# Epsilon inside the variance sums, scores on four quarters of the array, two columns more in one product, and another order of steps

## What is computed

```python
# layer 0: graph convolution, two dense layers, each with a norm over all 8192 rows
# layer 1: layernorm, attention with 4 heads, layernorm, MLP, layernorm
xp = einsum('mn,bnf->bmf', L_norm, x)
x1 = relu(_layernorm(xp @ Wc + bc, g1, be1)) + x
scores = einsum('bhnd,bhmd->bhnm', q, k) / sqrt(hd)        # hd = 64
attn = softmax(where(adjacency > 0, scores, -1e9))
o = einsum('bhnm,bhmd->bhnd', attn, v)
x2 = _layernorm(x1 + o @ Wo + bo, g2, be2)
y = _layernorm(x2 + gelu(x2 @ W1 + b1) @ W2 + b2, g3, be3)
# layer 2: two graph convolutions, then LSTMs over windows of 1, 2, 3, 4 nodes
# layer 3: graph attention
Wh = einsum('bnf,fo->bno', h, W)
s1, s2 = Wh @ a1, Wh @ a2
e = s1[:, :, None] + s2[:, None, :]        # leaky relu, mask, softmax
h_prime = einsum('bij,bjo->bio', attention, Wh)
# every layernorm: (x - mean) / sqrt(var + eps), here over 256 features
```

## Time and profile before

| | |
|---|---|
| median of three runs | 2094.58 us (2092.04 to 2097.44) |
| the profiled execution | 2096.32 us, of which the profile's span is 2094.5 us |
| PE busy | 1982.5 us, 95% |
| DVE busy | 1774.0 us, 85% |
| ACT busy | 1448.0 us, 69% |
| first and second part | 0 to 243 us |
| opening | 243 to about 373.6 us |
| seven rounds | about 225.5 us each, to 1951.9 us |
| closing | 1951.9 us to 2094.5 us |

### The profile page before, as it was taken

One profiled execution on the slowest core, in us unless ns is written; L12 is line 12 of the kernel. 1 busy time (PEld: TensorE's weight loads), 2 busy tenths in 40 slices (PEclk: granted clock), 3 DMA queues, 4 the chain that ended last, 5 costly groups with the idle time before them and its releaser, 6 DMA issues.

```text
span 2094.5 us, 86503 instructions
## 1 busy us (share of the span) xinstructions
PE 1982.5 (95%) x37415; PEld 1754.9 (84%) x37415; DVE 1774.0 (85%) x5049; ACT 1448.0 (69%) x4411; POOL 189.0 (9%) x252
## 2 busy tenths in 40 slices
PE   6999879999999999999999999999999999999997
PEld 3444469989898989899998989898989999899996
DVE  6769787889888988898888988898889888988866
ACT  5657436767776677767776777677776777677776
POOL 2000010110101000101011110101010101111000
PEclk9999989999999999999999999999999999999999
DMA  7847300000100001000100010000100010000000
GB/s 280 292 166 282 129 9 15 13 12 3 43 3 23 3 3 43 13 13 3 43 13 12 3 43 3 23 3 5 42 13 13 3 43 13 13 4 12 3 3 23
DMA packets 36825, 87.84 MB, mean 42 GB/s; under 512 B 2416, under 2 KB 26992, under 8 KB 32752
## 3 DMA queue, kind: packets, MB, share of 16 engines
q1 hardware_dynamic: 36464, 82.56, 11.4%
HBM read 52.15 MB, written 30.41 MB: 39 GB/s over the span
## 4 chain that ended last, share of the span: by engine, by line
PE 65%; DVE 14%; ACT 8%; issue 2%; POOL 0%; DVEq 0%; ACTq 0%
PE ps L283 19%; PE ps L285 18%; PE ps L284 18%; DVE stats L1610 2%; PE ps L297 2%; ACT pool_mem L1486 2%; PE ps L1226 2%; PE ps L1144 2%; PE ps L1135 1%; DVE pool_mem L1764 1%; ACT hl_a L1502 1%; DVE mv L1614 1%; PE ps L1381 1%; DVE t L1810 1%; PE ps L1251 1%
## 5 line engine op out<-in xcount | busy, mean ns | idle before, releaser
L1486 ACT ACTIVATE pool_mem<-ps,lstm_b 128x64 f32<-128x64 f32 (+2 forms) x2496 | 607.7, 357 | 95.6 <-PE ps L285 94.6
L283 PE MATMUL ps<-hl_a,w_hi 128*128 128x64 f16 (+2 forms) x3776 | 540.2, 214 | 16.9 <-DVE hl_a L654 15.9
L284 PE MATMUL ps<-hl_a,w_hi 128*128 128x64 f16 (+2 forms) x3776 | 539.3, 214 | 0.0
L285 PE MATMUL ps<-hl_a,w_lo 128*128 128x64 f16 (+2 forms) x3776 | 539.0, 214 | 0.0
L283 PEld LDWEIGHTS ps<-hl_a,w_hi 128*128 128x128 f16 x3776 | 349.1, 97 | 44.9 <-DVE hl_a L654 17.1
L285 PEld LDWEIGHTS ps<-hl_a,w_lo 128*128 128x128 f16 x3776 | 348.9, 97 | 23.7 <-issue 1.9
L284 PEld LDWEIGHTS ps<-hl_a,w_hi 128*128 128x128 f16 x3776 | 348.9, 97 | 22.6 <-issue 1.6
L283 PE MATMUL ps<-hl_b,w_hi 128*128 128x84 f16 (+2 forms) x2112 | 366.2, 228 | 1.0 <-DVE hl_b L1662 1.0
L284 PE MATMUL ps<-hl_b,w_hi 128*128 128x84 f16 (+2 forms) x2112 | 366.3, 228 | 0.0
L285 PE MATMUL ps<-hl_b,w_lo 128*128 128x84 f16 (+2 forms) x2112 | 364.4, 228 | 0.0
L284 PE MATMUL ps<-pool_mem,w_hi 128*128 128x64 f16 (+2 forms) x3072 | 351.1, 200 | 0.6 <-issue 0.6
(11 more groups left out here) (234 smaller groups left out, 4339.6 us busy)
## 6 DMA issues: line engine op xcount, KB each, us to landing
xa<-in_x SPq DMA_DIRECT2D x32, 512.0 KB, 5.5
h_scratch<-pool_mem SPq DMA_DIRECT2D x14, 1024.0 KB, 4.3
pool_mem<-h_scratch SPq DMA_DIRECT2D x14, 1024.0 KB, 7.0
...
```

Source lines behind the costliest of these rows:

```text
L283: nc.tensor.matmul(o, l[0], r[0], start=first, stop=False, skip_group_check=True)
L284: nc.tensor.matmul(o, l[0], r[1], start=False, stop=False, skip_group_check=True)
L285: return nc.tensor.matmul(o, l[1], r[0], start=False, stop=last, skip_group_check=True)
L1486: op = nc.scalar.activation(gates[s][h][:, g, m * w:(m + 1) * w], gate_place(s, h, g, m, w), ACT.Tanh, bias=lstm_b[:, bias:bias + 1], scal ...
```

## The change

Four things are changed.

**Epsilon.** The statistics buffer has nine columns a block instead of six. The three new ones hold 0, 0 and 256 x epsilon from the start on, and `bn_aggr` reads all nine, so that its variance comes out with epsilon in it. The addition on DVE is gone, and POOL takes the power of `mv` directly. The waits between `bn_stats`, `bn_aggr`, centring and scaling are now for each block instead of for both.

**Scores.** The second pair of heads writes to the opposite partitions and to the half's other bank, so that the 16 products use the four quarters in turn.

**Attention vectors.** They are stored as columns 256 and 257 behind the matrix W3 (`w3a`), and the 12 matmuls of `gat` have 258 columns. The 12 matmuls of two columns are gone. Block `b` of a half now has a bank to itself. ACT takes the parts out, in a new small instruction ahead of the copy of Wh, and the addition of DVE's L1785 is gone. `gat_keys` waits for the copy of Wh, because it writes into the bank that the copy reads.

**Order.** All three tables are written anew.

The core of the diff:

```diff
-        mask1 = sb("mask1", [P, NODES])
+        mask1 = sb("mask1", [P, P])
-        wa = sb("wa", [P, 2, KT, 2], F16)
+        w3a = sb("w3a", [P, 2, KT, DIM + 2], F16)
-        stats = [sb(f"stats_{s}", [P, BLK, 6]) for s in range(STREAMS)]
+        stats = [sb(f"stats_{s}", [P, BLK, 9]) for s in range(STREAMS)]
...
+                for s in range(STREAMS):
+                    nc.gpsimd.memset(stats[s][:, :, 6:8], 0.0)
+                    nc.gpsimd.memset(stats[s][:, :, 8:9], DIM * EPS)
...
+                for half, of in enumerate((w_hi, w_lo)):
+                    nc.vector.tensor_copy(w3a[:, half, :, 0:DIM], of[:, W_AT["w3"][0]:W_AT["w3"][0] + KT * DIM]
+                                          .rearrange("p (k d) -> p k d", k=KT))
...
             def scores_of(s, h):
-                return ps[s][:, BANK_B[h], :].rearrange("p (j k) -> p j k", j=SETS)
+                return ps[s][:, 2 * h:2 * h + PAIRS, 0:HTOK].rearrange("p q (b k) -> p b q k", b=HALF)
...
                     for b in range(HALF):
-                        for pair in range(PAIRS):
-                            for batch in range(BATCHES):
-                                at_b = b * P + batch * NODES
+                        for batch in range(BATCHES):
+                            at_b = b * P + batch * NODES
+                            for pair in range(PAIRS):
                                 for odd in range(2):
                                     d = slice(odd * HEAD_DIM, (odd + 1) * HEAD_DIM)
-                                    mm = nc.tensor.matmul(to[d, (b * PAIRS + pair) * BATCHES + batch, :],
+                                    half = slice((odd ^ pair) * NODES, ((odd ^ pair) + 1) * NODES)
+                                    mm = nc.tensor.matmul(to[half, b, pair, batch * NODES:(batch + 1) * NODES],
...
-                            mm = product(ps[s][:, BANK_B[h], HTOK + 2 * b:HTOK + 2 * b + 2],
-                                         (src[:, 0, k, a:a + P], src[:, 1, k, a:a + P]),
-                                         (wa[:, 0, k, :], wa[:, 1, k, :]), k == 0, k == KT - 1)
+                            mm = product(gat_bank(s, h, b)[:, 0:DIM + 2], (src[:, 0, k, a:a + P], src[:, 1, k, a:a + P]),
+                                         (w3a[:, 0, k, :], w3a[:, 1, k, :]), k == 0, k == KT - 1)
                     mm.then_inc(gat_ps.of(s, h), 1)
-                    dense(s, h, src, h * HTOK, "w3", BANK_A[h]).then_inc(gat_ps.of(s, h), 1)
...
-                    pe.wait_ge(*logit_ok.at(s, n, h, "parts"))
+                    pe.wait_ge(*taken.at(s, n, h, "wh"))
...
                 def take_wh(s, n, h):
+                    at = 8 + (s * HALVES + h) * HALF * 2
                     act.wait_ge(*gat_ps.at(s, n, h, "wh"))
-                    nc.scalar.activation(wh[s][h], tok(s, BANK_A[h]), ACT.Copy, scale=UNSCALE).then_inc(taken.of(s, h), 1)
+                    nc.scalar.activation(small[:, at:at + 2 * HALF].rearrange("p (b c) -> p b c", b=HALF),
+                                         ps[s][:, 2 * h:2 * h + HALF, DIM:DIM + 2], ACT.Copy, scale=-UNSCALE)\
+                        .then_inc(gat_ok.of(s, h), 1)
+                    nc.scalar.activation(wh[s][h], ps[s][:, 2 * h:2 * h + HALF, 0:DIM], ACT.Copy, scale=UNSCALE)\
+                        .then_inc(taken.of(s, h), 1)
...
-                    pool.wait_ge(*ln_ve.at(s, n, h, j))
-                    nc.gpsimd.tensor_tensor(rstd[s][:, blocks(h)], ve[s][:, blocks(h)], nhalf[:, 0:HALF], ALU.pow)\
+                    pool.wait_ge(*ln_mv.at(s, n, h, f"{j}.1"))
+                    nc.gpsimd.tensor_tensor(rstd[s][:, blocks(h)], mv[s][:, blocks(h), 1], nhalf[:, 0:HALF], ALU.pow)\
                         .then_inc(ln_rstd.of(s, h), 1)
...
-                    dve.wait_ge(*ln_step.at(s, n, h, f"{j}.mv"))
-                    nc.vector.tensor_scalar(ve[s][:, blocks(h)], mv[s][:, blocks(h), 1], EPS, None, ALU.add)\
-                        .then_inc(ln_ve.of(s, h), 1)
+                    for i in range(HALF):
+                        dve.wait_ge(*ln_step.at(s, n, h, f"{j}.t{i}"))
+                        b = h * HALF + i
+                        nc.vector.bn_stats(stats[s][:, b, 0:6], t[s][:, b, :]).then_inc(ln_step.of(s, h), 1)
+                    for i in range(HALF):
+                        dve.wait_ge(*ln_step.at(s, n, h, f"{j}.stats{i}"))
+                        b = h * HALF + i
+                        nc.vector.bn_aggr(mv[s][:, b, :], stats[s][:, b, :]).then_inc(ln_mv.of(s, h), 1)
```

Of the tables, the beginning of `ROUND` stands for the rest:

```diff
-1:cheb.1 0:pack3.1 0:cell3.0 1:conv.1 1:v.0 1:q.0 1:norm_g1.1 0:hid3.0 1:k.0 1:xa_bias.1 0:inp4.1 0:pack3.0
+1:cheb.1 0:pack3.1 0:cell3.0 0+norm_y 1:conv.1 0:inp4.1 0:hid3.0 1:norm_g1.1 0:cell4.1 1:v.0 0:pack3.0 1:q.0 1:k.0
```

More of the change, by code:

```diff
@@ L89 @@
-0:norm_l3.1 0:gat.0 0+turn_y.1 0:gat_keys.0 1:inp2.1 1:cell2.1 0+norm_l0.1 1:hid0.0 0:gat_exps.0 1:hid2.1 1:inp1.0
-0:turn_att.0 0+cheb.1 1:cell1.0 0:gat_mix.0 1:hid1.0 0:norm_l3.0 1:inp3.1 0+conv.1 0+turn_y.0 1:cell3.1 1:inp2.0
-0+norm_l0.0 1:cell2.0 0+norm_g1.1 0+cheb.0 1:hid2.0 1:inp3.0 0+xa_bias.1 0+turn_x1.1 0+conv.0 0+norm_g1.0 1:cell3.0
-0+xa_bias.0 0+v.1 0+q.1 0+k.1 0+turn_x1.0 1:hid3.0 0+scores.1 1:hid3.1 1:pack3.0 0+v.0 0+exps.1 0+q.0 0+k.0 1:pack3.1
-1:inp4.0 1:cell4.0 0+scores.0 0+turn_probs.1 1:hid4.0 1:inp4.1 0+attend.1 1:inp5.0 0+exps.0 1:cell4.1 1:cell5.0
@@ new lines @@
+0:gat_exps.1 1:gcn1.0 1:inp1.1 0:turn_att.1 1:cell1.1 0:gat_mix.1 1:hid1.1 0:gat.0 0:norm_l3.1 1:inp0.0 0+turn_y.1
+1:cell0.0 0:gat_keys.0 1:inp2.1 1:cell2.1 0+norm_l0.1 0:gat_exps.0 1:hid0.0 1:hid2.1 1:inp1.0 0:turn_att.0 0+cheb.1
+1:cell1.0 0:gat_mix.0 1:inp3.1 1:hid1.0 0:norm_l3.0 0+conv.1 0+turn_y.0 1:cell3.1 1:inp2.0 0+norm_l0.0 0+norm_g1.1
+1:cell2.0 0+cheb.0 1:hid2.0 0+xa_bias.1 1:inp3.0 0+conv.0 0+turn_x1.1 0+norm_g1.0 1:cell3.0 0+v.1 0+xa_bias.0 0+q.1
+0+turn_x1.0 1:hid3.0 0+k.1 1:hid3.1 0+scores.1 1:pack3.0 0+v.0 0+exps.1 0+q.0 1:pack3.1 0+k.0 1:inp4.0 1:cell4.0
@@ L105 @@
+0+hid2.1 0+inp3.1 1:norm_l3.1 1+norm_g1.0 0+inp2.0 0+cell2.0 1+turn_y.1 0+cell3.1 1+norm_l0.1 0+hid2.0 0+hid3.1
+0+inp3.0 1+xa_bias.0 1+turn_x1.0
 """.split()
@@ L115 @@
-0+mix0.0 1+norm_g1.0 0+gcn1.1 1+xa_bias.0 0+gcn0.0 0+mix1.0 0+inp0.1 0+cell0.1 0+hid0.1 0+gcn1.0 0+inp1.1 0+cell1.1
-0+inp0.0 0+hid1.1 0+cell0.0 1+turn_y.1 0+hid0.0 1+turn_x1.0 0+inp2.1 0+cell2.1 0+inp1.0 0+cell1.0 0+hid1.0 1+norm_l0.1
-0+hid2.1 0+inp3.1 0+inp2.0 0+cell2.0 0+cell3.1 0+hid2.0 0+hid3.1 0+inp3.0
+0+norm_y 0+turn_y.1 0+norm_l0.1 0+turn_y.0 0+cheb.1 0+norm_l0.0 0+conv.1 1+norm_y 0+norm_g1.1 0+cheb.0 0+xa_bias.1
+0+turn_x1.1 0+conv.0 0+v.1 0+q.1 0+norm_g1.0 0+k.1 0+xa_bias.0 0+scores.1 0+turn_x1.0 1+turn_y.0 0+exps.1 0+v.0
@@ new lines @@
+1+norm_l0.0 0+q.0 0+k.0 0+turn_probs.1 0+scores.0 0+attend.1 0+exps.0 0+attn_out.1 0+norm_g2.1 0+turn_probs.0
+0+attend.0 0+turn_x2.1 0+attn_out.0 0+mlp_up.1 0+norm_g2.0 0+gelu_split.1 0+turn_x2.0 1+cheb.0 0+mlp_down.1 0+mlp_up.0
+0+norm_g3.1 0+gelu_split.0 1+conv.0 0+norm_l1.1 0+mlp_down.0 0+mix0.1 0+norm_g3.0 0+norm_l1.0 0+gcn0.1 0+mix1.1
+0+mix0.0 0+gcn1.1 0+gcn0.0 1+norm_g1.0 0+mix1.0 0+inp0.1 0+cell0.1 0+hid0.1 0+gcn1.0 0+inp1.1 1+xa_bias.0 0+cell1.1
+0+hid1.1 0+inp0.0 0+cell0.0 1+turn_y.1 0+hid0.0 1+turn_x1.0 0+inp2.1 0+inp1.0 0+cell2.1 0+cell1.0 0+hid1.0 0+hid2.1
@@ L954, in build @@
             gelu_hi = Signal("gelu_hi", "m0 m1 m2 m3")
-            gat_ok = Signal("gat_ok", "logits exps out", ahead=1)
-            ln_step = Signal("ln_step", " ".join(f"{j}.{part}" for j in NORMS for part in ("t", "stats", "mv")))
-            ln_ve = Signal("ln_ve", " ".join(NORMS))
+            gat_ok = Signal("gat_ok", "parts logits exps out", ahead=1)
+            ln_step = Signal("ln_step", " ".join(f"{j}.{part}" for j in NORMS for part in ("t0", "t1", "stats0", "stats1")))
+            ln_mv = Signal("ln_mv", " ".join(f"{j}.{i}" for j in NORMS for i in range(HALF)))
             ln_out = Signal("ln_out", "l0 l1 l2 l3.nmr")
-            gained = Signal("gained", "g1.centred g1.scaled g2.centred g3.centred")
+            gained = Signal("gained", "g1.centred0 g1.centred1 g1.scaled g2.centred0 g2.centred1 g3.centred0 g3.centred1")
             x_ok = Signal("x_ok", "x1 x2")
```

200 lines of the change are left out of this document (97 added, 103 removed).

## The result

The changed kernel takes 2044.06 us in the median, beside 2094.55 us for the kernel before in the same comparison: 50.5 us less. One of its four executions took 4535 us, for a reason that no run here shows; the other three have a median of 2043.5 us, and the ratio 0.9756 (95% interval 0.9742 to 0.9769) is theirs. The prediction was 2069 us, 25.6 us less, with a range from 2050 to 2084.

A forecast was written before the change was run, and what follows sets the result against it. PE, busy 218.7 of 225.5 us in a round, was taken as the bound. The terms summed to -25.6 us, from the median of 2094.6 to 2069 us, with a range of 2050 to 2084 holding some 8 in 10.

The forecast's parts named there:

- The products themselves: PE's stream: 16 scores products at 0.63 us, gaining 0.50 a half; two-column matmuls gone, gaining 0.31 a half.
- The estimate of 0.73 us: Scores: if one bank takes only one row half at a time, the gain is 0.40 instead of 0.50 us.
- the rule of the Trainium skill: Scores: different row tiles cannot access the same PSUM bank at once; the sum would be about 3 us worse.
- The keys' new wait: Keys wait for ACT's copy of Wh, 1.15 us; only stream 0, half 1 is short, by 0.5 us: +3.5.
- The scores' wait behind k: Stream 0, half 1: nothing stands between k and scores in the new table, about 0.5 us a round, +3.5.
- Layernorms: Norm chains without DVE's addition: 0.2 us shorter at three PE waits a round, -4.2; opening -1.0; DVE's 38 us nothing.
- Waits that go: Graph and attention products: two PE waits shrink, another pair's grows; net -0.95 us a round, -6.6 in all.
- Other distances: New tables: shorter distances not priced singly, such as inp2 to inp3, add 0.5 us a round, +3.5.
- holes closed: Rival: the new order also fills half of a round's 6.8 idle us, 24 us more, 2045 us; chance 0.14.
- Opening and closing: Stretches outside the seven rounds: scores -1.0 over both, two-column matmuls -0.6 in the closing, norms -1.0 in the opening.

## Why the prediction was right, and where it failed

**The products themselves: right.** 0.63 us for the scores was the value taken, and it was measured at 0.63. The estimate of 0.73 us, for two row halves that take turns at one bank, did not come true. By the rule of the Trainium skill that the prediction weighed (page "TensorEngine Tiling (Array Packing)", section "Gotcha 1: PSUM Pressure"), the result would be 3 us worse. The trace does not bear it out: a pair of products on different row halves that write to different partitions of one bank loses nothing beside attend. The single records of the earlier trace rows, which the rows merge, point the same way: each of the two quarters starts a pass every 58 ns, the two 36 and 22 ns apart in turn, all into one bank, and in the changed kernel each of four quarters starts one every 58 ns too. A 128 column transpose in the same type follows another by 109 ns, so about 55 ns for 64 columns is, by estimate, the pace of a quarter that meets nothing. The run with scores in one bank for all 16 products, which would separate the banks from the quarters, was not made. The two-column matmuls and the scores are 3.2 us of a round, as summed. The whole scores edit brought 14.9 us in the new tables (-15.0 summed).

**The keys' new wait: right in mechanism, a little large in size.** The wait was 0.20 us where 0.5 was summed, since ACT's two copies overlap (0.07 us from start to start) and `mix1` covers 0.82 - 0.11 = 0.71 us where 0.63 was taken. In the tables of before the edit costs 15 us net, so covering this wait was the first thing that the order had to do. Counting what stands between Wh and the keys priced it well in the new tables; in the old ones it misses the half at which ACT is late. The scores' wait behind k grew by 0.44 us (0.5 summed).

**"Layernorms": the term that failed most.** It read -0.2 us at three places a round, -4.2, and -1.0 for the opening, with DVE's 38 us "which I count at nothing, since DVE isn't the bound". Measured alone the edit brings 17 us, and 39 in the order it was combined with. Three things in the step were wrong. The gain at each of the three places was 0.4 us and not 0.2: in the traces of the two kernels that split the edit, the three waits together go from 1.85 to 0.90 us without the addition, 0.3 each, and to 1.52 with the waits for each block, 0.1 each, to which the sum gave no price; alone they bring about 6 us. DVE's time is not worth nothing: a norm that PE doesn't wait for holds up DVE's next step of another half, and PE waited for such a step (the split `hl_b`), 0.38 us less now. With these the old tables' 1.4 us a round are accounted for, where the term had 0.6. And the places were counted in the old order, while the edit was to work in the new one, where the same waits are larger.

**"Waits that go" and "Other distances": the other failure.** The order was priced by PE's distances, with +0.4 us in all. Alone it costs 10.1 us, and with the three edits it brings 40.3. So the number asked for, what the order does, has no single value. Two effects in it can be named. The largest wait of the earlier trace rows, 1.2 us ahead of layer 3's attention product at one half, was in no term (the sum priced the 0.46 us of another half): the tables alone take the three places from 1.8 to 0.5 us, with long norms as with short ones. Against that, the waits behind a norm rise from 1.8 to 2.9 us in the kernel with the tables alone, and with the shorter norms they are 1.4 us. The shorter distances in the new table (3.1 to 0.9 us between `inp2` and `inp3`), which the prediction read as a likely cost, may be a part of that rise; no run separates them. By the table of prices the 40.3 us are the 22.5 us that epsilon is worth more in the new tables, 21.4 for the attention vectors and 6.3 for the scores, less the 10.1 of the tables alone. The rival "holes closed" had this size, 24 us, but its reasoning was only that holes are there, and it got 0.14: no working stands behind it, and that its 2045 us lie beside the measured time is luck.

**The range.** Its lower end of 2050 rested on that weight. The waits of a round had been bounded by the 6.8 idle us, and 2.6 of them went, well inside the bound. The error was in the chance, and in giving the epsilon edit one size, with nothing for DVE's saving.

**Opening and closing** lost 11.1 us where the sum had 2.6. With the epsilon edit alone the same stretches lose 7.3 us (4.7 and 2.6). That fewer chains cover one another there, so that a norm's latency is on the path more often, is the likely reason, but the clock has a part in it. The opening of the kernel before and of the changed one, the granted clock third from the end:

```profile
243.00:343.38 100.38, 78.09 (x1047) 64.91 (x1047) 75.68 (x199) 42.28 (x102) 10.30 (x13) 0.88 0.05 17
...
243.00:337.88 94.88, 72.33 (x1041) 61.95 (x1040) 72.90 (x174) 41.51 (x101) 9.45 (x13) 0.91 0.06 18
```

A mean of 0.88 is 24 us at 1.2 GHz in place of 2.4, one of 0.91 is 17 us, and the kernel with epsilon alone has 17 us too. PE was busy in 20 of the 24 us and in 14 of the 17. By my estimate from the two paces of a matmul above, up to 3 us of the opening's 5.5 (and of epsilon's 4.7) are the clock, and another 1.7 us in the closing, where the kernel before has 3.4 us at 1.2 GHz with PE busy (2071.1 us) and the other two have none. Whether the shorter waits kept the clock up or it fell by chance was not tested.

None of the other combinations was faster than the changed kernel; the nearest, with the old ends, is 2 us behind.
